# Chosen experts: the look-ups and slot counts of the last five experts are moved behind the first five groups' lower layers and biases

## The reference, cut to what matters

```python
logits = x_flat @ Wr                              # 12544 x 8
probs = jax.nn.softmax(logits, axis=0)            # over the tokens
vals, idx = jax.lax.top_k(probs.T, C)             # C = 1024 tokens for each expert
selected = x_flat[idx]
h = gelu(einsum('ecd,edf->ecf', selected, W1) + b1[:, None, :])      # 128 -> 512
out_e = einsum('ecf,efd->ecd', h, W2) + b2[:, None, :]               # 512 -> 128
output = zeros_like(x_flat).at[idx.reshape(-1)].add((vals[..., None] * out_e).reshape(-1, Dd))
```

## Time and profile before

| | |
|---|---|
| median of 3 runs | 1999.11 us (1997.42, 1999.12, 1999.11) |
| profiled execution, its own time | 1999.22 us |
| its span in the profile | 1997.5 us |
| mean granted TensorE clock | 0.92 of full |
| busy shares PE, DVE, ACT, POOL | 86%, 61%, 54%, 57% |
| stretch from the first gather to the last scatter's landing | 558.8 to 793.8 us |

### The profile page before, as it was taken

How to read it: one execution, slowest core, us unless ns; L and a number is a source line. 1 busy time by engine, 2 the same in 40 slices (tenths; PEclk the granted TensorE clock), 3 DMA queues, 4 the chain that set the end, 5 groups by cost and what they waited for, 6 DMA issues and landing times. The chain is left out here.

```text
span 1997.5 us, 44429 instructions
## 1 busy us (share of the span) xinstructions
PE 1710.8 (86%) x13083; PEld 1269.9 (64%) x13084; DVE 1225.8 (61%) x4791; ACT 1073.4 (54%) x2510; POOL 1139.8 (57%) x1040
## 2 busy tenths in 40 slices
PE   4999999995448874599999999999993899999996
PEld 2665556654426653266666767666662798998985
DVE  2889898883741000589999999999975122222221
ACT  2666666652415542366666666666641555555553
POOL 2455554431045886125566666665656487777776
PEclk8999999996558987699999999999996899999998
DMA  8988988952013333201111111111112576776774
GB/s 202 205 197 213 213 204 211 210 122 64 1 36 51 66 64 48 78 26 46 47 51 53 44 51 52 49 51 48 42 39 61 117 136 127 137 132 125 133 135 78
DMA packets 270772, 198.08 MB, mean 99 GB/s; under 512 B 25327, under 2 KB 251153, under 8 KB 270609
## 3 DMA queue, kind: packets, MB, share of 16 engines
q1 hardware_dynamic: 219536, 160.12, 31.9%
q0 software_dynamic: 49984, 35.38, 13.1%
q10 hardware_dynamic: 1088, 0.53, 0.1%
HBM read 143.33 MB, written 52.40 MB: 98 GB/s over the span
## 5 line engine op out<-in xcount | busy, mean ns | idle before, releaser
L2306 POOL DMA_INDIRECT out_dram<-r_yw,r_idx x212 | 328.5, 1549 | 116.9 <-issue 59.1
L2195 POOL DMA_INDIRECT rows_scratch<-routed_row,slot_u x256 | 252.3, 986 | 207.0 <-DVE slot_u L2146 143.5
L1868 ACT ACTIVATE a_probsT<-a_p_sc 98x392 f32<-98x392 f32 x384 | 174.2, 505 | 151.1 <-PE a_p_sc L1649 96.3
L2372 ACT ACTIVATE r_hT<-r_p_up,r_b1T 128x256 f32<-128x256 f32 x424 | 192.0, 475 | 116.2 <-PE r_p_up L2347 81.7
L2334 PEld LDWEIGHTS r_p_y<-w_all,r_hT 128*128 128x128 f32 x1696 | 225.1, 194 | 11.4
L2334 PE MATMUL r_p_y<-w_all,r_hT 128*128 x1696 | 225.9, 277 | 0.0
L2347 PE MATMUL r_p_up<-r_xgT,r_w1e 128*128 128x256 f32 x848 | 222.7, 386 | 0.6 <-ACT r_xgT L2377 0.6
L443 PE MATMUL p_embed<-pix,w_pix 96*128 96x392 f32 x512 | 211.1, 520 | 3.5 <-ACT pix L558 3.5
L2388 DVE TENSOR_TENSOR r_yb<-r_p_y,b_all 128x256 f32<-128x256 f32 x106 | 45.0, 425 | 191.3 <-PE r_p_y L2334 149.9
L1966 DVE TENSOR_REDUCE a_negmax<-a_p_max 98x2 bf16<-98x392 f32 x256 | 132.3, 559 | 46.2 <-PE a_p_max L1616 41.2
L708 POOL TENSOR_SCALAR vare<-mv 98x4 f32<-98x4 f32 x64 | 30.4, 475 | 221.6 <-DVE mv L693 192.5
(11 more groups left out here) (367 smaller groups left out, 4123.1 us busy)
## 6 DMA issues: line engine op xcount, KB each, us to landing
img<-in_x_dram SPq DMA_DIRECT2D x192, 196.0 KB, 4.2
img<-in_x_dram SPq DMA_DIRECT2D x192, 189.0 KB, 4.4
r_w1e<-in_L_ffn_W_dram SPq DMA_DIRECT2D x106, 256.0 KB
r_xg<-rows_scratch SPq DMA_DIRECT2D x106, 130.0 KB
xn_scratch<-xn SPq DMA_DIRECT2D x32, 196.0 KB
h_scratch<-h SPq DMA_DIRECT2D x32, 196.0 KB
h<-h_scratch SPq DMA_DIRECT2D x32, 196.0 KB
h3b<-h_scratch SPq DMA_DIRECT2D x32, 196.0 KB
```

The source lines that it names most:

```text
L1868: act.activation(probsT[:, u % 2, i, :], p_sc[i % 2][:, 0:2 * PAIR], ACT.Exp).then_inc(exped, 1)
L2195: pool.indirect_dma_start(rows_dram, bass.IndirectOffsetOnAxis(ap=slot_u[:, u % ROWS, c, t:t + 1], axis=0), row[:, u % ROWS, c, t, :], Non ...
L2306: pool.indirect_dma_start(acc_dram, bass.IndirectOffsetOnAxis(ap=idx[:, (k - 3) % 4, t:t + 1], axis=0), yw[:, (k - 3) % 4, t, :], None, co ...
L2372: act.activation(hT[:, (k - 1) % 2, f, :], p_up[f][:, 0:G], ACT.Silu, bias=b1T[:, bass.ds(e * FC + f, 1)]).then_inc(act_h, 1)
```

## The change

The five looks of experts 3 to 7 go to the ends of iterations 2 to 6 of TensorE's loop, each behind the lower layer of group n-2. The counts of an expert become a function `number(e)`; VectorE does experts 0 to 2 ahead, and `number(3 + u)` right behind the bias addition of group u, for u = 0 to 4. `mark_past(e + 2)` stays inside `number(e)`. The numbers of instructions are the same.

```diff
     AHEAD = 6
+    FIRST = AHEAD // PG
@@
-            for e in range(3):
+            for e in range(FIRST):
                 look(e)
-            places = {(0, FC): 3, (1, 2): 4, (1, FC): 5, (2, 2): 6, (2, FC): 7}
+            places = {(n, FC): n + 1 for n in range(FIRST - 1, EXPERTS - 1)}
@@
-            mark_past(0)
-            for e in range(EXPERTS):
+            def number(e):
                 for i in (2 * e, 2 * e + 1):
                     dve.wait_ge(looked, i + 1)
@@
                     if ahead < EXPERTS:
                         mark_past(ahead)
 
+            mark_past(0)
+            for e in range(FIRST):
+                number(e)
+
             for u in range(GROUPS):
@@
                 dve.tensor_tensor(yb[:, u % 2], p_y[:], b2e[:, s, :].unsqueeze(1).to_broadcast([128, GT, D]),
                                   ALU.add).then_inc(ybs, 1)
+                if FIRST + u < EXPERTS:
+                    number(FIRST + u)
```

## The result

| | before | after |
|---|---|---|
| median, us | 1999.12 (5 runs, 1997.42 to 2001.60) | 1990.15 (5 runs, 1983.59 to 1991.74) |
| profiled execution | 1999.22, span 1997.5 | 1983.59, span 1981.9 |

The ratio of the times is 0.9947, with a 95% interval of 0.9928 to 0.9967: 9.0 us faster by the medians, where 6.4 were forecast. The forecast of 1992.8 was 2.7 us too high; as a ratio it is 0.9968, just outside that interval. The profiled execution of after is the fastest of its five, and its distance to the one of before, 15.6 us, must not be read as the change's gain.

What follows compares the result with a forecast made beforehand. POOL, saturated with scatter and gather descriptors from scatter(1) on, was taken as the bound. Bias addition 1 coming 6.8 us earlier, less 0.4 for contention, gave 6.4 off 1999.2: 1992.8 us, bounds 1991.0 to 1993.9, stated range 1988 to 1998.

Steps and rivals of the forecast that it cites:

- Experts 0 to 2 unchanged, early gathers where they were: Up to 576 the same rows; POOL's six early gathers stay, ending at 588.77 + 0.94.
- The lower layer of group 0 starts 3.8 us earlier: TensorE begins it at 594.0, not 597.84, behind the gelu at 593.20, without two looks that waited for counts.
- I assume these stalls stay where they are: Late TensorE results, such as the 9.28 us gelu wait to 593.20, were assumed to stay put relative to POOL.
- From there to bias addition 0: Lower layer 0's start to VectorE's first bias addition: 594.0 to 603.9, where that addition stood at 609.78.
- The late end of my two bounds: Bias addition 0 at 604.4 if TensorE's clock stays low up to 599.75; the early end was 602.5.
- From bias addition 0 to 1: VectorE's first two bias additions 9.0 us apart, not 9.93: 8.59 plus 0.40 for expert 3's look.
- Sum from the gelu to scatter(1): Scatter(1) starts 6.4 us earlier: 6.8 at bias addition 1 less 0.4 for the comparisons.
- The moved counts are hidden: VectorE's number(3) needs 3.2 us in a gap of 8 between bias additions, so it costs nothing.
- Looks 4 to 7 in POOL's shadow: They cost TensorE 0.40 each, 1.6 us in sum, covered by POOL's queue; tightest slack 4.2 at scatter(3).
- Contention of the comparisons: Moved VectorE comparisons beside POOL's scatters and gathers lengthen POOL's chain by 0 to 1.0 us, taken as 0.4.
- Rival B: A count ahead of a bias addition waits 9 us for a stalled look; no change, 1998.4 us; chance 0.15.
- Rival A: TensorE's stall shrinks because looks of experts 3 and 4 left it; 1974 to 1990 us; chance 0.08.

Runs made afterwards that it cites:

- again2: The kernel after, unaltered, on the third chip: 1960.97 us, ratio 0.9966 to the kernel before on that chip.
- h_after: Kernel after, with ScalarE's last gelu of group 0 held until the sixth group's gather has landed: 1978.20 us, ratio 1.0054 to the kernel before.
- before_again: The kernel before, unaltered, on the third chip: 1964.35 us, ratio 0.9990 to the kernel before timed beside it.
- h_before: Kernel before, with ScalarE's last gelu of group 0 held until the sixth group's gather has landed: 1982.71 us, ratio 1.0070 to the kernel before.
- e5_three_early: Kernel after, with looks and counts of experts 3, 4 and 5 put back where they were: 1966.24 us, ratio 0.9993 to the kernel before.
- before3: The kernel before, unaltered, on the fourth chip: 1970.65 us, ratio 1.0008 to the kernel before timed beside it.

## Why the prediction was right, point by point

- **Experts 0 to 2 unchanged, early gathers where they were.** Right: from the first gather to the end of the last early one, 30.9 us before (558.80 to 589.71) and 30.5 after (554.17 to 584.70); the 0.4 us less is one gather, which lay beside the comparison of expert 5 at 573.85 and has none beside it now. It took 1.31 us before and 0.94 after. Before:

```profile
573.41 1.31 POOL L875 DMA_INDIRECT xg<-xn_scratch,tok_u  x1 [0.30 <-issue]
```

- **The lower layer of group 0 starts 3.8 us earlier.** Right relative to the gelu: 0.75 us behind it, against 4.64 before. The step "the last gelu of group 0, which ran at 593.20, stays" is the one that **failed**, as "I assume these stalls stay where they are". It came 7.0 us earlier behind the first gather in the profiled execution, which is the fastest of its five. Nothing ties this to the sum: it is luck, and it went the way that made the time lower. In the unheld kernels on three other chips the gelu came 19.0 to 20.3 us behind the first gather.
- **From there to bias addition 0: 9.9 us (594.0 to 603.9).** Measured 10.50 (582.34 to 592.84). TensorE ran at the low clock at first, as the first piece shows (2.07 us, as the 2.04 of a restart in the earlier trace rows, and 1.05 later). The granted clock was 0.74 in the stretch to 588.50, that is partly at 1.2 and partly at 2.4 GHz, and 1.00 in the next. The late end of my two bounds (10.4) was the better value. It also leaves out that TensorE waited for ScalarE twice on the way, 0.20 us for a gelu (587.24) and 0.63 for the copy (589.89), behind the table loads that the prediction had said would hide. In `again2`, without a restart at the low clock and with 0.23 us of such waits, the same stretch took 8.28 us, near the 8.5 that the prediction had for a high clock.
- **From bias addition 0 to 1: 9.0.** Measured 8.79, and 8.80 in `again2` and `h_after`; the look counted in it, and the wait of 1.95 went away, both as forecast.
- **Sum from the gelu to scatter(1): 6.4.** Measured 6.5 in the first pair, 5.9 in `before_again` and `again2` (26.57, 20.63), plus 0.6 from the gelu itself, 4.9 with the gelu held. By steps, in us, before and after:

| | first pair | `before_again`, `again2` | `h_before`, `h_after` |
|---|---|---|---|
| gelu to lower layer 0 | 4.64, 0.75 | 2.58, 0.74 | 0.74, 0.74 |
| gelu to bias addition 0 | 16.58, 11.25 | 13.61, 9.02 | 13.77, 10.32 |
| bias addition 0 to 1 | 9.93, 8.79 | 10.15, 8.80 | 10.25, 8.80 |

The first step of the prediction, 3.8 us at the lower layer, is there in full in the first pair alone; in `h_before` the looks were done while the gelu was held. The gain at bias addition 0 hangs less on it than on VectorE's own counts, which are all that this instruction waits for in the three traces of before.

- **The moved counts are hidden.** Right. VectorE waited 4.90 and 5.38 us for TensorE behind the first two blocks.
- **Looks 4 to 7 in POOL's shadow.** Right: no wait of POOL from scatter(1) to the last gather.
- **Contention of the comparisons, 0 to 1.0, taken 0.4.** Too high. The comparison at 595.86 took 0.88 and the scatter beside its start 1.70; but the same scatter of the kernel before took 1.63. The third comparison, at 613.95, lies beside a gather of 1.02 that is otherwise 0.94. The second, at 604.66, cost the scatter at 604.45 nothing (1.56). That is 0.15 us in sum. The rule of the Trainium skill ("SBUF — State Buffer", "Who interferes with whom") that I had weighed against it, a lock for a whole instruction, could cost up to the comparison's 0.75 us each time. No row shows that much; what agrees with it in kind is the gather at 573.41 above, 0.37 us longer than the others, which ended 0.12 us behind its comparison.
- **Rival B, a held-up look.** Seen in small, and without a price. A stall held bias addition 3 to 625.47 and, behind it, the second half of a count by 0.91 us (628.42, "remote"), where the rival had 9. Scatter(3) still followed scatter(2) without a wait of POOL, so the slack was enough. In `e5_three_early` a count that waited ahead of a bias addition did cost 2.4 us, and they reached the end, so the rival's mechanism is real and only its occasion didn't come.
- **Rival A.** A stall less gave 7.0 us of the first pair's 15.6, but nothing ties it to the change: where there was no stall, putting the two looks back moved the gelu by 1.2 us. The 2.7 us by which the forecast missed the median are within it. How much of the first chip's median gain of 9.0 is the mechanism and how much stall can't be split, since one execution of five was profiled.

What stays open: the cause of the stall, whether the order of the looks has a part in it where it occurs (none of the later chips had it, so neither was tried there), and what makes TensorE's clock fall late in the stage in one execution and not in another.

## What to carry to other kernels

Find the engine that is saturated up to the end of the stage, go back to the last wait ahead of that saturated run, and ask only how much earlier its releaser comes; then check the answer by adding up that engine's waits in several traces. A gain worked out step by step from one trace came within 0.1 us of that chip's traces here, and 0.5 and 1.5 us above the two other pairs. The place of a long "remote" wait can't be relied on like that: look at more than one execution, on more than one chip, before a sum leans on it. When work is taken from ahead of a critical instruction and put behind it, its own input must come an iteration earlier, or the next critical instruction stands behind it (`e5_three_early`, 2.4 us).

## What the runs showed of the hardware that I had not expected

- **TensorE's results are seen late in the first pair and not on three other chips.** There ScalarE's gelu waited 9.28 us and 9.05 us, "remote", for matmuls that the trace shows as ended (in the kernel after, those of 572.47, ended by 574.43, where the gelu came at 581.59), and VectorE's bias addition 3 of the kernel after 10.76 us; each of these waits began within a run of gathers. In this stage the two traces have eight and seven "remote" waits of ScalarE and VectorE, and the twelve later traces none. In the unheld kernels on three other chips the gelu waited 1.1 to 1.4 us, named as `p_up`, with the same gathers beside it. The cause isn't known. The same kernel took 1999.1 us in the first pair and 1968.3 to 1968.6 us on the others.
- **What an indirect scatter takes to land shows only when its cover is gone:** POOL waited 2.4 to 2.7 us for it where no gathers stood between.
- **TensorE often restarts at its low clock behind a wait.** The pieces of the lower layer at 582.34 and 626.31 after and at 610.61 before took 2.04 to 2.07 us, behind waits of 7.90, 5.31 and 1.95 us, and the granted clock was 0.50 in each of the three (1.2 GHz); in the running loop they took 1.05. A wait of 1.92 us late in `before_again` had no such effect (1.00), and in `before3` the clock fell only some way behind it (0.69).
